# Layer-1 weights issued behind the first gates, gates of the first four experts in four transfers, normalisation on VectorE, and the expert sum in three quarter-sized adds

## The reference

```python
x = x + 0.5 * L0_ffn(layernorm(x))    # MOE0_A: 16 experts, hidden 256, exact gelu, top 2
x = x + L0_attn(layernorm(x))         # ATT0:   linear attention over a sequence
x = x + 0.5 * L0_ffn(layernorm(x))    # MOE0_B: same weights
x = x + 0.5 * L1_ffn(layernorm(x))    # MOE1_A: 16 experts 128x128, relu, top 2
x = x + L1_attn(layernorm(x))         # ATT1:   causal linear attention, 16 heads
x = x + 0.5 * L1_ffn(layernorm(x))    # MOE1_B: same weights
```

## Time and profile before

| | us |
|---|---|
| median of 3 runs (lowest, highest) | 755.26 (754.49, 758.06) |
| the profiled execution | 756.41 |
| its span, first to last instruction | 754.7 |
| busy: TensorE, VectorE, ScalarE, GpSimd | 652.0, 486.9, 446.6, 223.7 |
| mean granted TensorE clock | 0.94 |

### The profile page before, as it was taken

How to read it: one execution, slowest core, us unless ns; L and a number is a source line. 1 busy time by engine, 2 the same in 40 slices (tenths; PEclk the granted TensorE clock), 3 DMA queues, 4 the chain that set the end, 5 groups by cost and what they waited for, 6 DMA issues and landing times.

```text
span 754.7 us, 7652 instructions
## 1 busy us (share of the span) xinstructions
PE 652.0 (86%) x2395; PEld 418.3 (55%) x2395; DVE 486.9 (65%) x1059; ACT 446.6 (59%) x899; POOL 223.7 (30%) x156
## 2 busy tenths in 40 slices
PE   3399998999899999999999998899999798557682
PEld 3266655656565655666565665466665465435451
DVE  4497348445754543588865565769865495699577
ACT  5357456647465854654667775584794457626483
POOL 2122010101011350230021254031164336765567
PEclk9789999999899999999999999899999879869797
DMA  8625331153225124222124320205130000000001
GB/s 243 172 63 114 60 98 38 29 115 56 58 56 93 24 54 111 57 53 61 56 57 93 71 61 12 46 2 112 56 58 0 1 0 1 0 14 1 0 1 42
DMA packets 26979, 42.23 MB, mean 56 GB/s; under 512 B 1641, under 2 KB 8890, under 8 KB 26938
## 3 DMA queue, kind: packets, MB, share of 16 engines
q1 hardware_dynamic: 26938, 41.74, 24.2%
HBM read 40.42 MB, written 1.31 MB: 55 GB/s over the span
## 4 chain that ended last, share of the span: by engine, by line
PE 48%; DVE 23%; POOL 14%; ACT 7%; issue 4%; SPq 2%; DMA 0%; POOLq 0%; DVEq 0%; ACTq 0%
PE py L1070 19%; POOL stage L426 5%; PE ph L855 5%; PE ph L856 5%; PE ph L857 5%; POOL stage L429 3%; POOL bc L426 2%; DVE stage L738 2%; POOL rstd L375 2%; DVE hw L814 2%; DVE stage L718 2%; DVE red L746 2%; ACT xn L462 1%; DVE stats L637 1%; PE pl L908 1%
## 5 line engine op out<-in xcount | busy, mean ns | idle before, releaser
L566 ACT ACTIVATE g<-ph,b1col 128x512 f32<-128x512 f32 x256 | 170.7, 690 | 137.1 <-PE ph L857 103.1
L1070 PE MATMUL py<-hw,w2s 128*128 128x512 f32 x512 | 247.6, 607 | 1.8 <-DVE hw L814 1.7
L814 DVE TENSOR_TENSOR hw<-g,bc 128x1024 f32<-128x1024 f32 x128 | 163.9, 1287 | 106.6 <-ACT g L566 101.2
L855 PE MATMUL ph<-xbh,w1h 128*128 128x512 f32 x256 | 140.0, 547 | 1.6 <-ACT g L566 1.6
L375 POOL TENSOR_TENSOR rstd<-vare,mhalf 128x4 f32<-128x4 f32 x24 | 35.2, 1468 | 354.1 <-DVE vare L643 354.1
L1070 PEld LDWEIGHTS py<-hw,w2s 128*128 128x128 f32 x512 | 95.9, 193 | 76.3 <-issue 64.5
L519 ACT ACTIVATE stage<-ps,comb 128x128 f32<-128x128 f32 x288 | 82.8, 513 | 33.3 <-PE ps L986 14.6
L856 PE MATMUL ph<-xbl,w1h 128*128 128x512 f32 x256 | 102.2, 399 | 0.0
L857 PE MATMUL ph<-xbh,w1l 128*128 128x512 f32 x256 | 101.9, 398 | 0.0
L426 POOL TENSOR_TENSOR stage<-stage 128x1024 f32<-128x1024 f32 x24 | 63.5, 2646 | 76.5 <-DVE stage L738 52.3
L855 PEld LDWEIGHTS ph<-xbh,w1h 128*128 128x128 f32 x256 | 49.5, 193 | 35.2 <-issue 24.8
(11 more groups left out here) (207 smaller groups left out, 962.9 us busy)
## 6 DMA issues: line engine op xcount, KB each, us to landing
bc<-comb_rows SPq DMA_DIRECT2D x32, 1024.0 KB, 8.4
stage<-in_L_ffn_W_dram SPq DMA_DIRECT2D x4, 512.0 KB, 6.6
X<-in_L_attn_x_dram SPq DMA_DIRECT2D x4, 256.0 KB, 3.2
out_dram<-X SPq DMA_DIRECT2D x4, 256.0 KB, 2.3
comb_rows<-combT SPq DMA_DIRECT2D x8, 32.0 KB, 7.5
side<-in_L_attn_wq_dram SPq DMA_DIRECT2D x1, 64.0 KB
side<-in_L_attn_wk_dram SPq DMA_DIRECT2D x1, 64.0 KB
side<-in_L_attn_wv_dram SPq DMA_DIRECT2D x1, 64.0 KB
```

The lines of the kernel that those rows point to most:

```text
L566: nc.scalar.activation(g[:, s % 2, h, 0:w], ph[:, (HC * s + h) % RING_PH, 0:w], ACT.Gelu, bias=b1col[:, HC * e + h:HC * e + h + 1]).then_i ...
L814: V.tensor_tensor(hw[:, s % RING_HW, :, 0:w], g[:, s % 2, :, 0:w], bc[:, s // GQ % 2, s % GQ, 0:w].unsqueeze(1).to_broadcast([P, HC, w]), ...
L855: T.matmul(dst, wh, xh, start=True, stop=False)
L1070: ins = T.matmul(py[:, 0:cols], w2s[:, w], hw[:, s2 % RING_HW, h, 0:cols], start=e2 == 0 and h == 0, stop=False)
```

## The change

The weights of layer 1 are issued after the second gate transfer of the first eight experts instead of before the first store of gates. The first gate transfer is cut into four, one for each expert, with a semaphore each. VectorE applies the normalisation itself, with one tensor_scalar for each tile (subtract the mean, multiply by rstd), so GpSimd's product and ScalarE's four activations go. VectorE writes its quarter of the expert sum as [e][d], without a stride; GpSimd adds blocks 0 and 1 as soon as ScalarE's three groups are there, then block 3, read with a stride, to block 2, then block 2 to block 0. The orders `LIGHT`, `HEAVY` and `TURNS` are new. In `LIGHT` chunk 3 of MOE0_A moves behind the first expert layers of the others: it is prepared around slot 52 instead of slot 4. In `HEAVY` the third chunk of ATT0 moves ahead of the first `f1`. In `TURNS` VectorE's first multiply (slot 0) stands behind the statistics and normalisation of chunk 2, where before it stood behind the router of chunk 1, the first step of `wt` and the statistics of chunk 3; `wt` now starts on VectorE behind slot 5 and on TensorE around slot 7; the last `f1` of MOE1_A (chunk 2) stands around slots 121 to 126 instead of 118 to 122, and the first step of ATT1 for chunk 2 behind the last slot instead of at slot 128 (on TensorE). GpSimd's power for the last normalisation stands before the fourth sum of MOE1_B chunk 2, and was behind it. The new `TURNS` strings are left out here.

```diff
-        rstd, nmean, nmr = (sb(n, [P, TPC]) for n in ("rstd", "nmean", "nmr"))
+        rstd = sb("rstd", [P, TPC])
...
+        bc_first = [sem(f"bc_first{e}") for e in range(GQ)]
...
-        LIGHT = (ln_rt_ct(MOE0_A, 0) + ln_rt_ct(MOE0_A, 1) + ln_rt_ct(MOE0_A, 3) + ln_rt_ct(MOE0_A, 2) +
-                 [("c0", MOE0_A, 0)] + [("ln", ATT0, 0)] + ln_rt_ct(MOE0_B, 0) + [("c0", MOE0_A, 1)] +
-                 [("ln", ATT0, 1)] + ln_rt_ct(MOE0_B, 1) + [("c0", MOE0_B, 0)] +
-                 [("ln", MOE1_A, 0), ("rt", MOE1_A, 0)] + [("c0", MOE0_A, 2)] + [("ln", ATT1, 0)] +
-                 [("ln", ATT0, 2)] + [("c0", MOE0_B, 1)] + ln_rt_ct(MOE0_B, 2) +
-                 [("ln", MOE1_B, 0), ("rt", MOE1_B, 0)] + [("ln", MOE1_A, 1), ("rt", MOE1_A, 1)] +
-                 [("c0", MOE0_A, 3)] + [("ln", ATT0, 3)] + [("ln", ATT1, 1)] + ln_rt_ct(MOE0_B, 3) +
-                 [("c0", MOE0_B, 2)] + [("ln", MOE1_A, 2), ("rt", MOE1_A, 2)] +
-                 [("ln", MOE1_B, 1), ("rt", MOE1_B, 1)] + [("ln", ATT1, 2)] + [("c0", MOE0_B, 3)] +
-                 [("ln", MOE1_A, 3), ("rt", MOE1_A, 3)] + [("ln", ATT1, 3)] +
-                 [("ln", MOE1_B, 2), ("rt", MOE1_B, 2)] + [("ln", MOE1_B, 3), ("rt", MOE1_B, 3)])
+        LIGHT = (ln_rt_ct(MOE0_A, 0) + ln_rt_ct(MOE0_A, 2) + ln_rt_ct(MOE0_A, 1) + [("c0", MOE0_A, 0)] +
+                 [("ln", ATT0, 0)] + ln_rt_ct(MOE0_B, 0) + [("c0", MOE0_A, 1)] + [("ln", ATT0, 1)] +
+                 [("c0", MOE0_B, 0)] + ln_rt_ct(MOE0_A, 3) + ln_rt_ct(MOE0_B, 1) + [("c0", MOE0_A, 2)] +
+                 [("ln", ATT0, 2)] + [("ln", MOE1_A, 0), ("rt", MOE1_A, 0)] + [("ln", ATT1, 0)] +
+                 ln_rt_ct(MOE0_B, 2) + [("c0", MOE0_B, 1)] + [("ln", MOE1_A, 1), ("rt", MOE1_A, 1)] +
+                 [("c0", MOE0_A, 3)] + [("ln", ATT0, 3)] + [("ln", ATT1, 1)] +
+                 [("ln", MOE1_B, 0), ("rt", MOE1_B, 0)] + ln_rt_ct(MOE0_B, 3) + [("c0", MOE0_B, 2)] +
+                 [("ln", MOE1_B, 1), ("rt", MOE1_B, 1)] + [("ln", MOE1_A, 2), ("rt", MOE1_A, 2)] +
+                 [("ln", ATT1, 2)] + [("c0", MOE0_B, 3)] + [("ln", MOE1_A, 3), ("rt", MOE1_A, 3)] +
+                 [("ln", ATT1, 3)] + [("ln", MOE1_B, 2), ("rt", MOE1_B, 2)] + [("ln", MOE1_B, 3), ("rt", MOE1_B, 3)])
         HEAVY = [("w1", MOE0_A, 0), ("q0", MOE0_A, 0), ("wt", MOE1_A, 0), ("a0", ATT0, 0), ("a0", ATT0, 1),
-                 ("f1", MOE1_A, 0), ("a1", ATT1, 0), ("a0", ATT0, 2), ("f1", MOE1_A, 1), ("a0", ATT0, 3),
+                 ("a0", ATT0, 2), ("f1", MOE1_A, 0), ("a1", ATT1, 0), ("f1", MOE1_A, 1), ("a0", ATT0, 3),
                  ("a1", ATT1, 1), ("f1", MOE1_A, 2), ("a1", ATT1, 2), ("f1", MOE1_B, 0), ("f1", MOE1_B, 2),
                  ("f1", MOE1_B, 1)]
...
-            sp.wait_ge(w1_ready, W1_PARTS)
-            sp.dma_start(stage[:, 0:E * D].rearrange("p (e h) -> p e h", e=E), expert_w.rearrange("e d h -> d e h")).then_inc(w_in["we"], 16)
-            for i, w in enumerate((Wq, Wk, Wv, Wo)):
-                sp.dma_start(stage[:, E * D + P * i:E * D + P * (i + 1)], w).then_inc(w_in["l1"], 16)
-            sp.dma_start(stage[0:E, E * D + 4 * P:E * D + 5 * P], gate_w).then_inc(w_in["l1"], 16)
-            sp.dma_start(be_raw, expert_b).then_inc(w_in["l1"], 16)
-
             for n, (l, c) in enumerate(MAIN):
...
                     if k >= 2:
                         sp.wait_ge(hw_ready, GQ * (k - 1))
+                    if k == 0:
+                        for e in range(GQ):
+                            sp.dma_start(bc[:, 0, e:e + 1, 0:wide(c)], comb_dram[l // 2, e:e + 1, col(c)].partition_broadcast(P)).then_inc(bc_first[e], 16)
+                        continue
                     sp.dma_start(bc[:, k % 2, :, 0:wide(c)], comb_dram[l // 2, q * GQ:(q + 1) * GQ, col(c)].partition_broadcast(P)).then_inc(bc_in[k % 2], 16)
+                    if k == 1:
+                        sp.wait_ge(w1_ready, W1_PARTS)
+                        sp.dma_start(stage[:, 0:E * D].rearrange("p (e h) -> p e h", e=E), expert_w.rearrange("e d h -> d e h")).then_inc(w_in["we"], 16)
+                        for i, w in enumerate((Wq, Wk, Wv, Wo)):
+                            sp.dma_start(stage[:, E * D + P * i:E * D + P * (i + 1)], w).then_inc(w_in["l1"], 16)
+                        sp.dma_start(stage[0:E, E * D + 4 * P:E * D + 5 * P], gate_w).then_inc(w_in["l1"], 16)
+                        sp.dma_start(be_raw, expert_b).then_inc(w_in["l1"], 16)
             last = [t[2] for t in LIGHT if t[0] == "ln" and t[1] == MOE1_B]
...
                 nc.gpsimd.tensor_tensor(rstd[:, 0:n], vare[:, 0:n], mhalf[:, 0:n], ALU.pow).then_inc(light["rstd"], 1)
-                pool.wait_ge(light["rstd"], nth_light("rstd", l, c))
-                nc.gpsimd.tensor_tensor(nmr[:, 0:n], nmean[:, 0:n], rstd[:, 0:n], ALU.mult).then_inc(light["nmr"], 1)
...
                 r = rel_late if late else rel
                 for j in range(ntiles(c)):
                     pool.wait_ge(signal["relu_a"], (n + j + 1) * ACT_GROUPS)
+                    r0, r1, r2, r3 = (r[:, j % 2, a * E * D // 4:(a + 1) * E * D // 4] for a in range(4))
+                    nc.gpsimd.tensor_tensor(r0, r0, r1, ALU.add).then_inc(signal["half"], 1)
                     pool.wait_ge(signal["relu_v"], (n + j + 1) * (GROUPS - ACT_GROUPS))
-                    lo, hi = (r[:, j % 2, a * E * D // 2:(a + 1) * E * D // 2] for a in range(2))
-                    nc.gpsimd.tensor_tensor(lo, lo, hi, ALU.add).then_inc(signal["half"], 1)
-                    pool.wait_ge(signal["half"], n + j + 1)
-                    l4, h4 = (lo.rearrange("p (a n) -> p a n", a=2)[:, a, :] for a in range(2))
-                    nc.gpsimd.tensor_tensor(l4, l4, h4, ALU.add).then_inc(signal["quarter"], 1)
+                    nc.gpsimd.tensor_tensor(r2.rearrange("p (d e) -> p d e", d=D), r2.rearrange("p (d e) -> p d e", d=D),
+                                            r3.rearrange("p (e d) -> p d e", d=D), ALU.add).then_inc(signal["half"], 1)
+                    pool.wait_ge(signal["half"], 2 * (n + j + 1))
+                    nc.gpsimd.tensor_tensor(r0, r0, r2, ALU.add).then_inc(signal["quarter"], 1)
...
             def ln(l, c):
-                act.wait_ge(light["nmr"], nth_light("nmr", l, c))
-                full = l not in (MOE1_A, MOE1_B)
-                for j in range(ntiles(c)):
-                    rows = slice(PIECES[c][0] * D + j * D, PIECES[c][0] * D + (j + 1) * D - (not full))
-                    ins = nc.scalar.activation((xn if full else xn1)[:, j * D:(j + 1) * D - (not full)], X[:, rows], ACT.Identity,
-                                               bias=nmr[:, j:j + 1], scale=rstd[:, j:j + 1])
-                ins.then_inc(light["xn"], 1)
+                yield
                 yield
                 act.wait_ge(light["xt_ps"], nth_light("xt_ps", l, c))
                 nc.scalar.activation(xbh[:, col(c)], pl[:, 0:wide(c)], ACT.Copy).then_inc(light["xh"], 1)
...
-                V.tensor_scalar(nmean[:, 0:n], mv[:, 0:n, 0], -1.0, None, ALU.mult)
                 V.tensor_scalar(vare[:, 0:n], mv[:, 0:n, 1], LN_EPS, None, ALU.add).then_inc(light["stat"], 1)
+                yield
+                dve.wait_ge(light["rstd"], nth_light("rstd", l, c))
+                full = l not in (MOE1_A, MOE1_B)
+                for j in range(ntiles(c)):
+                    rows = slice(PIECES[c][0] * D + j * D, PIECES[c][0] * D + (j + 1) * D - (not full))
+                    ins = V.tensor_scalar((xn if full else xn1)[:, j * D:(j + 1) * D - (not full)], X[:, rows],
+                                          mv[:, j, 0:1], rstd[:, j:j + 1], ALU.subtract, ALU.mult)
+                ins.then_inc(light["xn"], 1)
                 yield
                 dve.wait_ge(light["xh"], nth_light("xh", l, c))
...
-                            V.scalar_tensor_tensor(r[:, j % 2, :].rearrange("p (a d e) -> p a e d", a=4, d=D)[:, q],
+                            V.scalar_tensor_tensor(r[:, j % 2, q * CH:(q + 1) * CH].rearrange("p (e d) -> p e d", d=D),
                                                    banks[:, u % 3, :].rearrange("p (e d) -> p e d", d=D), 0.0,
                                                    comb[:, PIECES[c][0] + j, 4 * q:4 * q + 4].unsqueeze(2).to_broadcast([P, 4, D]),
                                                    ALU.max, ALU.mult).then_inc(signal["relu_v"], 1)
...
-                    if s % GQ == 0:
-                        dve.wait_ge(bc_in[s // GQ % 2], 16 * (s // GQ // 2 + 1))
+                    if s < GQ:
+                        dve.wait_ge(bc_first[s], 16)
+                    elif s % GQ == 0:
+                        dve.wait_ge(bc_in[s // GQ % 2], 16 * ((s // GQ + 1) // 2))
```

2 lines of the change are left out of this document (1 added, 1 removed), and 36 rows, old and new, of the table TURNS.

## The result

| | before | after |
|---|---|---|
| median us (lowest, highest) | 755.26 (754.49, 758.06) | 762.09 (760.66, 762.80) |
| ratio, 95% interval | | 1.007 (1.0036, 1.0104) |
| span of the profiled execution | 754.7 | 759.7 |
| first hw multiply | 40.94 | 28.22 |
| hw multiply of slot 16 | 94.77 | 86.37 |

The slot rows are the starts of the hw multiply (L814 before, L820 after) in the timeline of VectorE. They split the time in three: the start won 8.4 us by slot 16, slots 16 to 127 gave back 10.7 (503.4 us for 492.7), and the tail cost 2.8 more. I had predicted -8, -1 and -7.

The account below looks back on a forecast made before the run. TensorE, busy 652 of 754.7 us, was taken as the bound, its idling lying at the two ends. Start -8, middle -1 and tail -7 gave -16 to -17: 738 us from 755.3, own range 731 to 746, overall 727 to 750.

Parts of the forecast that it names:

- The middle, forecast as -1, bounds -6 to +4: Twelve expert-sum tiles under the slots: at most 6.7 us of TensorE idling to recover; -1 us taken.
- TensorE full at both places: Chunk 3's first experts, moved from the start to slot 52: TensorE busy at either place, so 0.
- TensorE has two slots of lag (6 us) against 1.9 us of pow: Beside the experts: hw multiplies queued on DVE behind its wait for pow would not hold up TensorE.
- same work: Moving chunk 3's first experts to slot 52 leaves the amount of work unchanged, priced at 0.
- My 1.9 us from the variance on: Normalisation chain from variance to first transpose: pow 1.02, hop 0.1, operations 0.7, 0.1; 1.9 us instead of 3.2.
- The middle stretch gets longer by over 4 us: Sign that would make the prediction wrong: the middle takes over 4 us longer than before.
- The start, -8: Up to the first slots: first multiply at 28 instead of 40.94 us, less work displaced; -8 us, bounds -4 and -12.
- The normalisation, -2.6 in the tail, nothing in the slots: Normalisation moved to VectorE: -1.3 us for each of two tail places, -2.6; worth nothing under the slots.
- The expert sum, -3.3, -3, +2 and a share of the middle: Late tiles of MOE1_A -3.3 us, MOE1_B chunks 0 and 2 -3, last eight tiles +2; middle tiles within -1.
- The case against the strided read: GpSimd's strided add some 50% dearer per element, estimated 1.9 us; 20 tiles lose about 5 us, giving 743.
- The order's -3 and +3: Tail: earlier GpSimd power for the last normalisation -3 us; later normalisation and projections of attention chunk 2 +3.
- The slower rival that I gave 0.06: GpSimd's strided add costs far more than on DVE across 20 tail tiles; 770 us at x = 2; chance 0.06.

Follow-up runs that it names:

- e_old_order: The whole change, but with the order of before from slot 14 on; 752.24 us, ratio 0.9933 against the kernel before.
- e_start_alone: The kernel before with only the start of the change (split first gates, later weights, new order of the start's steps); 755.89 us, ratio 0.998.
- e_after_loose2: The changed kernel with four normalisations (slots 18, 25, 34, 54) at the old spacing, their router and attention steps moved along; 755.72 us, ratio 0.9964.
- e_tight: e_old_order with normalisations beside the experts drawn together: transposes, copy and difference earlier, VectorE's normalising step half a slot later; 768.51 us, ratio 1.0142.
- e_tight_pe: e_old_order with only the transposes half a slot earlier, copy and difference one slot earlier, normalising step left in place; 762.79 us, ratio 1.0078.
- e_norm_slots: The kernel before with VectorE's normalisation beside the experts and ScalarE's for the five in the tail; 758.79 us, ratio 0.9989.

## Why the prediction was wrong

**The middle, forecast as -1, bounds -6 to +4, was +10.7.** This is the step that failed. I read "TensorE full at both places" and "TensorE has two slots of lag (6 us) against 1.9 us of pow", and priced the order by how much work it moves, not by how close it puts a consumer behind its producer. Two things were wrong in it. First, chunk 3's preparation, "same work", 0, was no zero: the start's -8 is the time up to a mark that this work used to lie ahead of, so its 3.7 us had to be charged in the middle. Second, the lag that counts is that of the transposes: 1.5 slots behind the statistics in the place of 2, and TensorE is there after 4.1 us, where the chain takes 4.65. My 1.9 us from the variance on was 3.2, as long as what I had read before: power 1.93 (I took the 1.02 of a place without a multiply of VectorE beside it), operations 1.12 (I took 0.7, against an upper bound of 0.87). The runs show the size: the same edits with the old order and spacing 0.993; with transposes, copy and difference early 1.008; and four of the changed kernel's normalisations respaced bring 1.06% back. Against the kernel before, the transposes wait only 2.1 us more: the new order gives away room that the shorter chain had made, for in e_old_order they don't wait at all. "The middle stretch gets longer by over 4 us" stood among the things that would make the prediction wrong, and it was that.

**The start, -8.** At slot 10 it was -8.5 after, and -8.3 in e_start_alone, and the first multiply came at 28.22 for 28.2. But as a part of the total it is 0.998, 1.5 us, not told from 0. I had charged chunk 1's share of the old wait and priced chunk 3's move at 0. The measured share: two slots after slot 10, where that run prepares its fourth chunk, 4.5 of the 8.3 are gone. So the -8 at its mark was right in part because one chunk less was ready there. Of the 2 us that its trace loses between slots 16 and 127 and the 2 more in the tail I have no cause.

**The normalisation, -2.6 in the tail, nothing in the slots.** Nothing in the slots is right where the spacing is kept (0.999). In the tail of before it is +7.9 on the profile: VectorE carries the loop there, and I charged it neither the wait for the power in its queue nor its own 1.1 us. I had named the queue ("DVE now also waits for pow") and looked only at the multiplies behind it. In the changed kernel's own tail it is neutral, by the one run on it: there four operations beside GpSimd's additions take 3.9 and 4.0 us, and why ScalarE's version, without them, is no faster is not shown.

**The expert sum, -3.3, -3, +2 and a share of the middle.** Direction and terms are right: 0.68 for 0.69, 0.30 for 0.38, the last eight tiles 4.15 us apart (4.2). The part is worth -7.5 alone, where my terms gave -4 and something from the middle; of that, 3.8 us are in slots 16 to 127, so the idling there was recovered after all, and the tail's -1.7 is less than my -4.3. The case against the strided read, 50% by the Trainium skill (GPSIMD Engine Reference, Performance pitfalls for Q7 kernels), did not come: 1579 against 1283 ns is +23%, a two-source add of which one source is strided.

**The order's -3 and +3** were not measured singly; together they were -1.8 in the traces (170.0 for e_old_order's 171.8). The tail as a whole was +2.8 for -7. The slower rival that I gave 0.06 was the strided add; a slower case by missing room between engines was not on my list.

What is left open: whether the other half of the new order (chunk 3 at slot 52, the crowded stretches 64 to 80 and 98 to 112) costs or brings anything with full spacing; e_after_loose2 (495.2 from slot 16 to 127, with the chunk's 3.7 us in it) is 4 us behind e_old_order there, and 0.3% in all, which the intervals don't tell apart. And what carries the loss: TensorE's wait at the transposes, ScalarE's copy and gelus behind it, or the lower granted clock. The wait is about as long as the loss in e_tight and e_tight_pe, too short for it in e_after_loose2, and e_norm_slots gains nothing by losing most of it.

The best of the runs keeps start and sum and the order of before: 746.6 (0.984), or 743.8 (0.984) with VectorE's normalisation beside the experts only; the ratios don't tell the two apart.

## What to carry to other kernels

When an order of steps is written out over several engines, count for every hand-over the time from the producer's first input to its last output, in the place where it runs, and compare it with the distance to the consumer in the new order; half a slot too little, at an engine that is otherwise full, cost some 11 us here over seventeen hand-overs, and at a single one, where the producer also came to stand beside GpSimd's additions, 4.5 more. When work moves past the mark at which a gain is read, charge it on the other side. Before you read a variant of an order, compare each engine's instructions in the traces: half a slot on an engine that has nothing in that half changes nothing. Time freed at the start counts only after subtracting what the waiting engine used to do in it. Work moved off a slack engine onto the one that carries the tail costs its duration and the wait at its head, even if it gets faster by the move.
